# Four column tiles in the first attention, pairs of row tiles in the second, and a new timetable beside the LSTM

## The reference, cut to what matters

```
c = cond_block(x, cond)       # adaLN, 16-head softmax attention (heads of 8), hyperbolic maps, FFN 128-512-128
x = x + causal_attention(c)   # 16 heads of 8, 256 positions, softmax over earlier positions
h = lstm(x, h0=cond)          # 256 steps one after the other; a = x_t @ Wx + h @ Wh + b (4 gates of 128)
out = x + ffn(h)              # 128-512-128, exact gelu
```

## Time and profile before

| what | us |
|---|---|
| median of 3 runs (646.81 to 648.69) | 648.4 |
| the profiled execution, its own time | 646.27 |
| its span in the trace | 644.5 |
| front | 0 to 58.4 |
| first attention, first half | 58.4 to 91.4 |
| second half, beside side chain 0 | 91.4 to 127.3 |
| rest of side chain 0 | 127.3 to 157.3 |
| chunk 0 of the second attention | 157.3 to 177.7 |
| 256 LSTM steps | 177.7 to 636.2 |
| tail | 636.2 to 644.5 |

### The profile page before, as it was taken

One profiled execution on the slowest core, in us unless ns is written; L12 is line 12 of the kernel. 1 busy time (PEld: TensorE's weight loads), 2 busy tenths in 40 slices (PEclk: granted clock), 3 DMA queues, 4 the chain that ended last, 5 costly groups with the idle time before them and its releaser, 6 DMA issues.

```text
span 644.5 us, 16323 instructions
## 1 busy us (share of the span) xinstructions
PE 489.7 (76%) x6317; PEld 383.3 (59%) x6317; DVE 385.3 (60%) x2265; ACT 239.7 (37%) x928; POOL 20.5 (3%) x31
## 2 busy tenths in 40 slices
PE   2546986784867599978468888998998986687776
PEld 1225764573756376867446766766766665566664
DVE  8896237538577655467756566566666754544442
ACT  1357645524334324233333343343333333332332
POOL 8030000000000000000000000000000000000000
PEclk9567996886555555565555555555565555556555
DMA  6200000000000000000000000000000000000000
GB/s 186 73 0 1 3 2 2 1 2 1 1 2 3 2 1 1 2 2 3 2 1 3 2 3 2 2 3 1 3 2 2 3 2 2 8 8 5 6 6 8
DMA packets 8824, 5.71 MB, mean 9 GB/s; under 512 B 1988, under 2 KB 8236, under 8 KB 8748
## 3 DMA queue, kind: packets, MB, share of 16 engines
q1 hardware_dynamic: 7564, 3.77, 2.2%
q10 hardware_dynamic: 1184, 0.92, 0.5%
HBM read 4.15 MB, written 0.52 MB: 7 GB/s over the span
## 4 chain that ended last, share of the span: by engine, by line
PE 44%; DVE 33%; ACT 16%; issue 5%; DMA 1%; PEldq 0%; ACTq 0%; DVEq 0%
PE bank L1622 14%; PE bank L1478 6%; ACT h_fac L762 6%; DVE h_off L1298 5%; ACT gates L760 5%; DVE pr L1291 4%; PE bank L1398 4%; DVE gates L1294 4%; DVE h_fac L1292 2%; DVE mx L1237 2%; PE bank L1518 2%; DVE pt_mla L1247 2%; PE bank L1446 2%; PE bank L1380 2%; PE bank L1460 2%
## 5 line engine op out<-in xcount | busy, mean ns | idle before, releaser
L1622 PEld LDWEIGHTS bank<-h_off,wha 128*128 128x128 f16 x1020 | 52.0, 109 | 145.2 <-DVE h_off L1298 135.8
L1622 PE MATMUL bank<-h_off,wha 128*128 128x4 f16 x1020 | 68.9, 172 | 84.0 <-DVE h_off L1298 80.0
L760 ACT ACTIVATE gates<-bank 128x16 f32<-128x16 f32 x256 | 47.2, 185 | 181.2 <-PE bank L1622 181.0
L1291 DVE SCALAR_TENSOR_TENSOR pr<-gates 128x8 f32<-128x8 f32 x256 | 41.5, 162 | 112.4 <-ACT gates L760 111.6
L1478 PE MATMUL bank<-kT,qz 32*128 32x32 f32 (+7 forms) x256 | 105.8, 534 | 0.0
L762 ACT ACTIVATE h_fac<-gates 128x4 f32<-128x4 f32 x256 | 53.1, 207 | 120.2 <-DVE gates L1294 120.2
L1298 DVE TENSOR_TENSOR h_off<-h_fac 128x4 f16<-128x4 f32 x256 | 43.1, 169 | 63.5 <-ACT h_fac L762 63.2
L1478 PEld LDWEIGHTS bank<-kT,qz 32*128 32x128 f32 x256 | 63.6, 311 | 3.1 <-issue 1.1
L1622 PE MATMUL bank<-h_low,wha 128*128 128x4 f16 x1020 | 63.4, 167 | 0.0
L1622 PE MATMUL bank<-h_off,whb 128*128 128x4 f16 x1020 | 62.7, 166 | 0.0
L1300 DVE TENSOR_TENSOR_SCAN h_low<-h_fac,h_off 128x12 f16<-128x12 f32 x256 | 46.6, 182 | 8.7
(11 more groups left out here) (279 smaller groups left out, 764.9 us busy)
## 6 DMA issues: line engine op xcount, KB each, us to landing
x_tm<-in_x ACTq DMA_DIRECT2D x1, 512.0 KB, 5.4
x_tb<-in_x SPq DMA_DIRECT2D x4, 128.0 KB, 2.6
wf<-in_L_cond_w_f SPq DMA_DIRECT2D x2, 256.0 KB, 3.4
out_y<-tb SPq DMA_DIRECT2D x7, 64.0 KB, 1.9
ada_w<-in_L_cond_w_ada SPq DMA_DIRECT2D x1, 384.0 KB
ada_b<-in_L_cond_b_ada ACTq DMA_DIRECT2D x1, 384.0 KB, 5.9
w1s<-in_L_ffn_w SPq DMA_DIRECT2D x1, 256.0 KB
w2s<-in_L_ffn_w SPq DMA_DIRECT2D x1, 256.0 KB
```

What stands on the lines that cost most here:

```text
L760: nc.scalar.activation(gates[:, k, 0:GW], src, ACT.Tanh, scale=1.0 / A_SCALE).then_inc(gates_act, 1)
L1291: V.scalar_tensor_tensor(pr[:, k, :], gates[:, k, B:3 * B], 1.0, gates[:, k, 3 * B:5 * B], ALU.add, ALU.mult).then_inc(p_ready, 1)
L1622: ins = T.matmul(acc[:, g * B:(g + 1) * B], w[:, g, :], h, start=False, stop=True, skip_group_check=True)
```

## The change

In the first attention `values` takes two units at once, with all four column tiles, and the extra semaphore for a finished group goes. In the second attention two neighbouring head groups form a pair: their score matmuls alternate between two row tiles and two banks, one mask matmul serves all batches of a unit, and for c >= 4 four banks are used, so that the values of all four batches are issued together on four column tiles, in two halves. Pairs follow every 7, 5 or 6 steps. The v product, the "up" matmuls, the norms and L1460 are cut into smaller pieces, the timetable and the last FFN's steps are set anew, and the preparation of `wh`, `wha`, `whb`, `h0` and the product `h0 @ wh` move ahead of chunk 0.

```diff
-        pt_mla = sb("pt_mla", [P, 2, 512])
+        pt_mla = sb("pt_mla", [P, 4, 512])
-        hist = sb("hist", [P, S, B])
+        hist = vaug[:].rearrange("p t h v -> p (t h v)")[:, 0:S * B].rearrange("p (t b) -> p t b", b=B)
...
             if c < 4:
-                return u, (0, 1, 2, 3)
-            g, bp = divmod(u, 2)
-            return g, (2 * bp, 2 * bp + 1)
-        UNIT_EVERY = 3
-        SCORES_FROM = 7
-        VALUES_AFTER = 8
+                return u, (0, 1, 2, 3), 3 + u % 2, u % 2
+            gp, bp, odd = u // 4, u // 2 % 2, u % 2
+            return 2 * gp + odd, (2 * bp, 2 * bp + 1), (3, 0)[bp] + odd, 2 * bp + odd
+        PAIR_EVERY = (7, 7, 7, 7, 5, 6, 6, 6)
+        SCORES_FROM = 8
+        def values_at(c, i):
+            for q in range(unit_count(c) // 2):
+                j = i - pair_from(c, q) - 8
+                if c < 4 and 0 <= j < 2:
+                    return 2 * q + j, 0, c + 1
+                if c >= 4 and q % 2 and 0 <= j < 4:
+                    cut = (c + 2) // 2
+                    return 2 * (q // 2) + j // 2, (0, cut)[j % 2], (cut, c + 1)[j % 2]
-        INPUTS_AT = {STEPS - 4: (0, 3), STEPS - 3: (3, 5), STEPS - 2: (5, 7), STEPS - 1: (7, 9)}
+        INPUTS_AT = {STEPS - 4: (0, 2), STEPS - 3: (2, 4), STEPS - 2: (4, 6), STEPS - 1: (6, 9)}
-        CHUNK_FROM = {1: 0, 2: 20, 3: 40, 4: 64, 5: 88, 6: 112, 7: 136}
+        CHUNK_FROM = {1: 0, 2: 18, 3: 40, 4: 72, 5: 94, 6: 119, 7: 144}
-        PE_AT = dict(projected=30, v_turned=33, up0=34, up1=37, up2=39, up3=43, normed=45)
+        PE_AT = dict(projected=30, v_turned=33, up0=35, up1=38, up2=41, up3=47, normed=51)
-        FFN_FROM = free_steps[CHUNK_FROM[7] + values_end(7)] + 2
-        FFN_EVERY = 8
+        FFN_FROM = free_steps[CHUNK_FROM[7] + values_end(7)] + 3
+        FFN_EVERY = 6
...
 ACT: behind side 0's "third"
+            for g0, g1, f in ((0, 3, .5), (3, 4, 1.)):
+                nc.scalar.mul(wh[:, g0:g1, :], wh[:, g0:g1, :], W_SCALE * f).then_inc(w_ready, 1)
+            act.wait_ge(w_ready, 6)
+            nc.scalar.activation(flat(wha[:]), flat(wh[:]), ACT.Copy).then_inc(w_ready, 1)
+            nc.scalar.mul(h0[:], condT[:], H_SCALE).then_inc(w_ready, 1)
...
 DVE: one pair's maxima at its steps 2 and 3, its four transposes at 4 to 7; v's mask product at i = 8 and 9
...
 PE, first attention
+            def values(q):
+                k, g, bp, _ = UNITS[2 * q]
+                pe.wait_ge(exp_done, 2 * q + 2)
...
                 for i in range(4):
-                    for j in (2 * jp, 2 * jp + 1):
+                    for j in range(GROUP):
                         ins = T.matmul(bank[VP * j:VP * j + VP, to, bb * P:(bb + 1) * P], vaug[...],
-                                       p_cond[w % 6][...],
+                                       p_cond[(2 * q + j // 2) % 6][...],
                                        start=(kc == 0), stop=(kc == 1), tile_position=(0, VP * j), skip_group_check=True)
...
 PE, side chain: two matmuls of 256 columns for each of 512; a yield behind each f of the norms and in the middle of each c of L1460
...
 PE, second attention
                 for i in range(len(bs) // 2 * part, len(bs) // 2 * (part + 1)):
+                    for g, _, at, _ in pair:
+                        rows = slice(32 * g, 32 * g + 32)
+                        T.matmul(bank[:, at, i * n:(i + 1) * n], qz[rows, ...], kT[rows, bs[i], 0:n], ..., tile_position=(32 * g, 0))
                 if part:
+                    for g, _, at, _ in pair:
+                        T.matmul(<the last 32 columns of every batch>, sel32[rows, :], <mask32 for every batch>, ...).then_inc(ms_mm, 1)
...
-            for i in range(chunk_span(0)):
+            pe.wait_ge(w_ready, 9)
+            for g in range(4):
+                T.matmul(bank[:, 6, g * B:(g + 1) * B], wh[:, g, :], h0[:], start=False, stop=True, skip_group_check=True)
+            for i in (*range(6), 8, 9, 6, 7, *range(10, chunk_span(0))):
                 attend(0, i)
-            inputs_of(0, range(5, 9))
-            pe.wait_ge(w_ready, 9)
+            inputs_of(0, range(5, 9)).then_inc(gates_mm, 1)
```

More of the change, by code:

```diff
@@ L724, in attend @@
                                          ACT.Copy).then_inc(mqk_ready, 1)
-                for after, part in ((3, 0), (4, 1)):
-                    u, w = divmod(i - SCORES_FROM - after, UNIT_EVERY)
-                    if w == 0 and 0 <= u < unit_count(c):
-                        m_exp(c, u, part)
+                for q in range(unit_count(c) // 2):
+                    j = i - pair_from(c, q) - 3
+                    if 0 <= j < 4:
+                        m_exp(c, 2 * q + j // 2, j % 2)
                 if i == values_end(c) + 3:
@@ L1396, in values, with pairs @@
                     bb, kc = 2 * bp + i // 2, i % 2
-                    for j in (2 * jp, 2 * jp + 1):
+                    for j in range(GROUP):
                         ins = T.matmul(bank[VP * j:VP * j + VP, to, bb * P:(bb + 1) * P], vaug[:, HALVES * bb + kc, GROUP * g + j, :],
-                                       p_cond[w % 6][:, 512 * (j % 2) + i * P:512 * (j % 2) + (i + 1) * P],
+                                       p_cond[(2 * q + j // 2) % 6][:, 512 * (j % 2) + i * P:512 * (j % 2) + (i + 1) * P],
                                        start=(kc == 0), stop=(kc == 1), tile_position=(0, VP * j), skip_group_check=True)
                 ins.then_inc(pv_mm, 1)
-                if w % PER_GROUP == PER_GROUP - 1:
-                    pe.wait_ge(pv_mm, w + 1)
-                    pe.sem_inc(pv_group, 1)
-            def units(first, last):
-                for w in range(first, last):
-                    if w + 2 < len(UNITS):
-                        scores(w + 2)
-                    values(w)
+            def pairs(first, last):
+                for q in range(first, last):
+                    for w in (2 * q + 2, 2 * q + 3):
+                        if w < len(UNITS):
+                            scores(w)
+                    values(q)
             def side(k):
@@ L1464, in side, with m_scores @@
                 yield "end"
-            def m_scores(c, u, part):
-                m = unit_base(c) + u
-                g, bs = unit_of(c, u)
+            def m_scores(c, q, part):
                 n = STEPS * (c + 1)
+                pair = [unit_of(c, 2 * q + odd) for odd in range(2)]
                 if part == 0:
-                    if u == 0:
+                    if q == 0:
                         pe.wait_ge(mqk_ready, c + 1)
-                    if m >= 2:
-                        pe.wait_ge(mp_ready, 2 * m - 2)
-                rows = slice(32 * g, 32 * g + 32)
+                    free = bank_free(c, 2 * q + 1)
+                    if free > 0:
+                        pe.wait_ge(mp_ready, 2 * free)
+                bs = pair[0][1]
@@ new lines, in m_values @@
+            def m_values(c, g, first_kb, end_kb):
+                n = STEPS * (c + 1)
+                us = [u for u in range(unit_count(c)) if unit_of(c, u)[0] == g]
+                if first_kb == 0:
+                    pe.wait_ge(mt_ready, 2 * (unit_base(c) + us[-1]) + 2)
+                    if g == 0:
+                        pe.wait_ge(mv_ready, 2 * c + 2)
+                        if c:
+                            pe.wait_ge(moT_ready, c)
+                for kb in range(first_kb, end_kb):
+                    for u in us:
+                        _, bs, _, place = unit_of(c, u)
+                        for i, b in enumerate(bs):
+                            ins = T.matmul(bank[32 * b:32 * b + 32, 5, g * GROUP * VW:(g + 1) * GROUP * VW],
+                                           pt_mla[:, place, i * n + kb * STEPS:i * n + (kb + 1) * STEPS],
+                                           vbd[:, b, kb, GROUP * g:GROUP * (g + 1), :].rearrange("p j v -> p (j v)"),
+                                           start=(kb == 0), stop=(kb == c), skip_group_check=True, tile_position=(0, 32 * b))
+                if end_kb == c + 1:
+                    ins.then_inc(mpv_mm, 1)
@@ L1519, in attend @@
                                            start=True, stop=True, skip_group_check=True, tile_position=(0, 32 * j))
-                    ins.then_inc(mv_mm, 1)
-                for part in range(2):
-                    u, w = divmod(i - SCORES_FROM - part, UNIT_EVERY)
-                    if w == 0 and 0 <= u < unit_count(c):
-                        m_scores(c, u, part)
-                u, w = divmod(i - SCORES_FROM - VALUES_AFTER, UNIT_EVERY)
-                if w == 0 and 0 <= u < unit_count(c):
-                    m_values(c, u)
+                    if i == 7:
+                        ins.then_inc(mv_mm, 1)
+                for q in range(unit_count(c) // 2):
+                    j = i - pair_from(c, q)
+                    if 0 <= j < 2:
+                        m_scores(c, q, j)
+                taken = values_at(c, i)
+                if taken:
+                    m_values(c, *taken)
```

(4 more changed lines are left out.)

138 lines of the change are left out of this document (65 added, 73 removed).

## The result

The changed kernel takes **620.2 us** (median of 4 runs, 619.4 to 620.9); the kernel before, run beside it, took 647.6 (643.5 to 648.7). The ratio is 0.960, 95% interval 0.956 to 0.964. 619 had been predicted. The profiled execution took 620.17 us with a span of 618.3, against 644.5 before: 26.2 us less. The two traces say where they come from, and that is less tidy than the total.

The account below looks back on a forecast made before the run. No engine was taken as full overall: PE nearly fills the first attention's first half, and LSTM steps carry 50.5 us of excess. Terms -6.1 - 3.8 - 2.3 - 17 = -29 take 646.3 to 617, median 619 us, range 609 to 626.

Parts of the forecast that it names:

- rival 2: First attention: with less to do PE is granted only 1.2 GHz throughout, +9 and +2 behind, 630 us; chance 0.15.
- First half, -6.1: First attention's first half: four column tiles make ACT the bound, groups 4.5 us instead of 6.1; bounds 0 and -8.
- Second half, -3.8: First attention's second half: side chain 0's 2.64 us DVE wait for ACT goes, about 1 more; bounds -2.6 and -5.
- The clock, 0 in the sum: First attention: the forecast sum had no term for a lower PE clock, which stood only as rival 2.
- whb, +0.9: Side chain 0's second join: POOL making whb in 1.15 us slows a DVE operation on the path, +0.9 us.
- h0 and chunk 0, -3.2 together: Ahead of the first tanh: moved h0 product gains 1.7, gives back 0.6; paired scores in chunk 0 gain 2.1.
- Row tiles overlap in float32: Second attention's scores: full overlap assumed, a pair of parts taking the 1.0 to 1.2 us of one, not 2.1.
- rival 1: Second attention's scores: float32 row tiles do not overlap and chunk 0 gains nothing, +26, 645 us; chance 0.10.
- Rival 3: Second attention's scores (L1478): row tiles exclude one another, each change of tile costs a drain, 660 us; chance 0.03.
- The ranges of the LSTM, 33.3 of excess: LSTM's five step ranges: excess over 1.60 us a step falls from 50.5 to 33.3 us, -17; bounds -25 and +7.
- Rival 4: LSTM: a side chain 1 semaphore arrives a step late, recurrence gains 7 instead of 17, 629 us; chance 0.17.
- rival 5: Whole kernel: no change, step gains eaten by new meetings and first attention stays as it is; chance 0.02.

Follow-up runs that it names:

- the fillers: Changed kernel plus unread 128 x 512 float16 matmuls in TensorE's waits in the first attention's second half: 618.5 us with 26, 615.7 us with 40.
- the two-tile order: Changed kernel with each 32 value instructions of the first attention run through column tiles 0 and 1, then 2 and 3: 619.9 us, ratio 0.960.
- the fuller fillers: Changed kernel plus 40 unread matmuls in the first attention's second half, 18 in place of 10 ahead of unit 31: 615.7 us, ratio 0.954.

## Why the prediction was right, point by point

**The total** was 619 and came out at 620.2. That is closer than the working behind it: between the profiled executions 29 us were forecast (646.3 to 617) and 26.1 measured (to 620.2), and the 2.1 us added for the median, which the changed kernel did not show (its profiled execution is its median), covered most of the rest. Ahead of the LSTM 12.2 us were forecast and 7.9 measured; the LSTM was to give 17 and gave 18.3. The largest miss is the clock's place in the sum: it stood as rival 2 with a chance of 0.15 and a price of its own, at nothing in the forecast, and part of it happened.

- **First half, -6.1.** Measured -7.5 (L1079 7.8 earlier, of which 0.3 came with the front). Groups 4.2 us apart, not 4.5. The mechanism was right: 32 instructions on four tiles take 1.01 us, as 16 on two did (1.07), and ACT's exponentials nearly closed up. What the prediction did not price by itself is the wait: the order over the tiles is worth 0.6 of 1.7 us a group, and 1.1 come with 32 instructions behind one wait, in which the tiles overlap in part in either order.
- **Second half, -3.8.** Measured -4.0 (from -7.8 to -11.7), and DVE's wait of 2.64 us is gone. But with the first attention undone 2.6 of the 4.0 stay: the wait is 1.32 us there, and the clock is back at 1.0 14.6 us behind L1079 in place of 17.2. So this hit is in part luck, since only 1.4 us go with the cause that was named.
- **The clock, 0 in the sum.** Measured +4.4 between the turn of v and L1214: the first half of the up projection 3.78 in place of 1.98 us, the norms 5.46 in place of 3.73, the values between them 1.68 in place of 1.07 and from the turn of v to the up projection 1.86 in place of 1.40; the down projection took 5.34 and before 5.44, and lost nothing. Rival 2 had looked for it in the values and the scores of the first attention; it fell mostly on the float32 matmuls behind them. That the clock is the price is shown by the fillers; that less work for PE is what lowered it, as rival 2 has it, is not.
- **whb, +0.9.** Measured +1.0, at L988, and shown by moving it.
- **h0 and chunk 0, -3.2 together.** Measured -1.6: chunk 0 18.5 in place of 20.4 us, and 0.3 given back ahead of it. The missing part is DVE's order: the prediction let v fill the wait of the last unit, and did not see that DVE's own program puts v's products ahead of the maxima. Reordering gave 2.55.
- **Row tiles overlap in float32.** Right, and it was the largest single bet: rival 1 is refuted at 2.07 against 1.22 us a pair part, and its +26 was if anything too small (+30). Rival 3, a drain at each change of tile, is refuted by the same rows.
- **The ranges of the LSTM, 33.3 of excess.** Measured 32.2. Steps 33 to 68 were 2.4 better than forecast. Steps 69 to 127 were 1.8 worse; 1.0 of that stands in steps 69 and 70, just behind the edge of the range before, 0.6 in step 78, and step 108 cost 1.14 (forecast 0.85). Steps 39 and 42 cost 0.97 and 1.43, forecast 0.9 each; v in halves was worth 5.3 by experiment; steps 220 to 223 cost 3.67 (forecast 3.1).
- **Rival 4**, a semaphore a step late over and over, did not happen but for the two squares that had been forecast; **rival 5** neither. The 0.1 us for a change of tiling mode was not measured by itself.

## What to carry to other kernels

When an edit takes work from TensorE on a path where it waits for others, look up the granted clock in the windows behind the edit, not in it: the next long float32 matmuls may run at the lower clock (3.78 us in place of 1.99 here), and unread matmuls in the gaps, 40 to 44 here, can hold the clock up. Column and row tiles pay where their instructions stand together behind one wait and alternate; where a change of this kind is possible, compare busy time of the same group in both orders before counting on it. After a change of order on one engine, read the other engines' programs against it: here 2.5 us hung on DVE asking for its operands in the old order, and 1.5 on two squares asked for one step early.

## What the runs showed of the hardware

- Float32 matmuls of different column tiles need not start in the order of the program: with two tiles at a time the first ones of tiles 2 and 3 started at 72.25 us, ahead of six of tiles 0 and 1 that stand before them.
- A DVE operation of 0.16 us took 1.16 beside one of 1.15 on POOL.
- The same total can hide two effects of 3 us that cancel out: the two-tile order lost 2.9 us at L1079 and had it all back by the first tanh, with the up projection at the full clock.
- Steps 220 to 223 differ between kernels in which nothing near them was edited. In the changed kernel they run at a granted clock of 0.50 and have 3.67 us of excess. In the kernel with the first attention undone the clock rose there, and the four steps (the first at 557.09) read:

```profile
557.09:559.50 2.41, 2.41 (x20) 1.92 (x20) 0.78 (x6) 0.39 (x2) 0.00 (x0) 0.50 0.12 34
559.50:561.58 2.08, 2.08 (x21) 2.07 (x22) 0.78 (x6) 0.39 (x3) 0.00 (x0) 0.64 0.02 4
561.58:563.30 1.72, 1.72 (x22) 1.47 (x22) 0.78 (x6) 1.29 (x7) 0.00 (x0) 1.00 0.00 0
563.30:564.90 1.60, 1.60 (x23) 1.44 (x23) 0.78 (x6) 0.41 (x3) 0.00 (x0) 1.00 0.00 0
```

  2.81 and 2.64 us in the third and fourth step became 1.72 and 1.60. It happened in three of the kernels, with the two-tile order and the fuller fillers as well, and accounts for about 2 us of their times. Which executions get it was not tested; a guess is that it depends on when this dense stretch begins. A difference of 2 us between totals of such kernels therefore says nothing until these steps have been compared.
- Nine kernels with the changed kernel's own program up to L1079 reached it between 82.8 and 85.3 us, with the granted clock rising and falling at other places. A shift of a mark ahead of the LSTM is therefore not better known than to some 2 us, unless the stretches around it are compared as well: the 2.9 us of the fuller fillers are 19.8 in place of 22.7 between two marks, with the first of them at the same place. The steps of the LSTM repeat within 0.05 us where the clock is the same.
